# Layer 0 of a relational graph network: eight relation weights made once on the chip, multiplied with scaled sums kept in two buffers

## What is computed

```python
W = jnp.einsum('rb,bde->rde', comp, basis)      # 8 relation weights from 4 bases
h = jnp.einsum('nd,rde->nre', x, W)
msg = h[src, edge_type]
sums = segment_sum(msg, dst * R + edge_type, n * R)
cnt  = segment_sum(ones, dst * R + edge_type, n * R)
agg  = (sums / maximum(cnt, 1)).reshape(n, R, -1).sum(axis=1)
return agg + x @ root + bias
```

## Time and profile before

| what | us |
|---|---|
| median of 3 timed executions | 5880.24 (5867.17 to 5891.92) |
| span of the profiled execution, first to last instruction | 4574.0 |
| layer 0, first to last gather issued | 126.72 to 2251.02 |
| first gather of layer 1 | 2297.41 |
| mean granted TensorE clock (1 is 2.4 GHz) | 0.788 |

### The profile page before, as it was taken

How to read it: one execution, slowest core, us unless ns; L and a number is a source line. 1 busy time by engine, 2 the same in 40 slices (tenths; PEclk the granted TensorE clock), 3 DMA queues, 4 the chain that set the end, 5 groups by cost and what they waited for, 6 DMA issues and landing times.

```text
span 4574.0 us, 121525 instructions
## 1 busy us (share of the span) xinstructions
PE 3738.4 (82%) x38021; PEld 3272.6 (72%) x38022; DVE 3166.8 (69%) x8385; ACT 892.6 (20%) x2493; POOL 3246.8 (71%) x3382
## 2 busy tenths in 40 slices
PE   2476677777767767767549999999999999999999
PEld 2355555555555555555438999999999999999998
DVE  6577677777777777776646767676676767677674
ACT  5000000000000000000003333333333333333333
POOL 1677777777777777777567777777777777777770
PEclk6565665665656656655559999999999999999999
DMA  6666655565555555555466666565656566656661
GB/s 211 181 194 195 174 168 168 165 168 168 165 168 168 164 168 166 167 168 164 122 170 173 173 173 169 170 171 168 169 168 172 167 172 174 170 170 168 171 171 21
DMA packets 359003, 762.96 MB, mean 167 GB/s; under 512 B 130103, under 2 KB 182108, under 8 KB 358657
## 3 DMA queue, kind: packets, MB, share of 16 engines
q0 software_dynamic: 215360, 663.86, 51.3%
q1 hardware_dynamic: 129381, 81.62, 6.6%
q10 hardware_dynamic: 14112, 16.06, 1.0%
HBM read 725.50 MB, written 35.78 MB: 166 GB/s over the span
## 4 chain that ended last, share of the span: by engine, by line
PE 57%; DVE 20%; issue 12%; POOL 6%; DMA 3%; ACT 1%; DVEq 0%; POOLq 0%; SPq 0%; ACTq 0%
PE bank L1469 15%; PE bank L1482 15%; PE bank L1382 12%; DVE mixed L1015 7%; DVE inv L1048 6%; POOL slot L593 5%; PE bank L1414 4%; PE bank L1378 4%; PE bank L1444 3%; PE bank L1445 2%; DVE scaled L1055 2%; DVE hot L1030 2%; DMA slot<-table,idx 2%; DVE inv L1047 1%; DVE mixed L1013 1%
## 5 line engine op out<-in xcount | busy, mean ns | idle before, releaser
L593 POOL DMA_INDIRECT slot<-table,idx x3354 | 3234.9, 965 | 1191.5 <-issue 979.4
L1382 PE MATMUL bank<-hot,slot 128*128 (+1 forms) x21168 | 1252.5, 213 | 62.7 <-DMA slot<-table,idx 54.1
L1382 PEld LDWEIGHTS bank<-hot,slot 128*128 128x128 bf16 x21168 | 1002.3, 108 | 125.2 <-issue 68.6
L1378 PE MATMUL bank<-hot,ones_b 128*128 x1764 | 401.3, 227 | 650.0 <-DVE scaled L1055 225.1
L1378 PEld LDWEIGHTS bank<-hot,ones_b 128*128 128x128 bf16 x1764 | 181.4, 103 | 936.0 <-issue 877.9
L1469 PE MATMUL bank<-root_sb,ffn_w 128*128 128x128 f32 x6272 | 772.9, 278 | 0.0
L1482 PE MATMUL bank<-ffn_w,act 128*128 128x256 f32 x3136 | 756.7, 384 | 1.0 <-DVE root_sb L1142 0.7
L1469 PEld LDWEIGHTS bank<-root_sb,ffn_w 128*128 128x128 f32 x6272 | 741.4, 192 | 8.0
L1482 PEld LDWEIGHTS bank<-ffn_w,act 128*128 128x128 f32 x3136 | 569.5, 190 | 64.9 <-issue 1.1
L1015 DVE SCALAR_TENSOR_TENSOR mixed<-scaled,small,mixed 128x256 f32<-128x256 f32 x1372 | 573.7, 481 | 12.2
L1015 DVE SCALAR_TENSOR_TENSOR mixed<-scaled,comp_sb,mixed 128x256 f32<-128x256 f32 x1372 | 573.4, 480 | 10.5
(11 more groups left out here) (158 smaller groups left out, 2407.5 us busy)
## 6 DMA issues: line engine op xcount, KB each, us to landing
slot<-table,idx POOLq DMA_INDIRECT x3354, 3.1
inv<-inv_d SPq DMA_DIRECT2D x98, 256.0 KB
table<-ffn_w SPq DMA_DIRECT2D x7, 1344.0 KB, 5.5
table<-parts ACTq DMA_DIRECT2D x49, 192.0 KB, 2.9
ffn_w<-in_L_ffn_W_dram SPq DMA_DIRECT2D x16, 512.0 KB, 5.3
typed_x_d<-zn ACTq DMA_DIRECT2D x49, 128.0 KB, 3.2
zn<-in_x_dram SPq DMA_DIRECT2D x48, 128.0 KB
root_sb<-typed_x_d SPq DMA_DIRECT2D x48, 128.0 KB
```

What stands on the lines that cost most here:

```text
L593: gp.indirect_dma_start(out=slot[:, k, :], out_offset=None, in_=table[layer], in_offset=bass.IndirectOffsetOnAxis(ap=idx[:, h, k:k + 1], a ...
L1378: t.matmul(C[:, at], ones_b[:, :], oh, start=(k == 0), stop=(k == TILES - 1), skip_group_check=True)
L1382: last = t.matmul(S[f][:, at], slot[:, k, q * D + f * P:q * D + (f + 1) * P], oh, start=(k == 0 and q == 0), stop=(k == TILES - 1 and q == ...
```

## The change

Three things change in layer 0; layer 1 keeps its mixes.

`make_relations` on DVE, once, after the first two `one_hots`: for each of the eight relations it makes W_r from four bases, by eight products and 24 multiply-adds of 128x512 f32. The bases of layer 0 are loaded into the place of the typed map's weights (`linw_sb`), and the eight results go to `basis_sb` (four), `mixed` (two) and `act` (two), which layer 0 now has free. The typed map's weights are loaded later, after the experts.

`transform` of layer 0 multiplies `scaled` itself with the eight weights: 2 x 2 x (1 + 8) = 36 matmuls in place of 20. It waits for `sc_ready` of its pair in place of `mixed_ready`.

`scale` of layer 0 writes pair p into buffer p & 1 of `scaled` and no longer waits for `mixed_ready`; `mix_bases` is gone from layer 0.

```diff
+            def make_relations():
+
+                dve.wait_ge(basis_in[0], 16)
+                for b in range(NBASIS):
+                    for r in range(R):
+                        s = comp_sb[0][:, r * NBASIS + b:r * NBASIS + b + 1]
+                        w = relation(r, slice(0, HALVES), slice(0, D))
+                        if b == 0:
+                            ins = v.tensor_scalar(w, basis0_sb[:, b, :, :], s, None, ALU.mult)
+                        else:
+                            ins = v.scalar_tensor_tensor(out=w, in0=basis0_sb[:, b, :, :], scalar=s, in1=w,
+                                                         op0=ALU.mult, op1=ALU.add)
+                    if b < NBASIS - 1:
+                        ch.link(ins)
+                ins.then_inc(relations_ready, 1)
...
             def scale(layer, h, G, p, at=0):
                 summed(dve, G, h)
+                at = bass.ds(p & 1, 1) if layer == 0 and not isinstance(p, int) else slice(at, at + 1)
...
                     scale(0, 1, p, p)
                     save(p - 1)
-                    mix_bases(0, p)
                     if more:
                         one_hots(1, p + 1)
                     bias_mask(p)
...
             def transform(layer, G, p):
-                pe.wait_ge(mixed_ready, G + 1)
                 if layer == 0:
+                    pe.wait_ge(relations_ready, 1)
+                    pe.wait_ge(sc_ready, p * 2 + (START + 2))
                     pe.wait_ge(relu_done, START + p)
...
+                            t.matmul(T[:, cols], root_sb[:, 0, k, cols], featT[:, k, bass.ds(p * P, P)],
+                                     start=(k == 0), stop=False)
+                            for r in range(R):
+                                last = t.matmul(T[:, cols], relation(r, k, cols), scaled[:, at, k, r, :],
+                                                start=False, stop=(k == HALVES - 1 and r == R - 1))
```

More of the change, by code:

```diff
@@ L1001, in general_sums, with mix_bases @@
                     assert chg.n == 3
-            def mix_bases(layer, G, first=0, last_=MIXES, at=0):
+            def make_relations():
[12 more added lines that the diff above has]
+                ins.then_inc(relations_ready, 1)
+            def mix_bases(G, first=0, last_=MIXES, at=0):
                 if first == 0:
-                    if not isinstance(G, int) or G > 0:
-                        dve.wait_ge(tr_done, G)
+                    dve.wait_ge(tr_done, G)
                     dve.wait_ge(sc_ready, G * 2 + (START + 2))
@@ L1050, in scale @@
                     dve.wait_ge(inv_in[h], p * 16 + 16)
[L1051 to L1053 removed]
+                if h == 0 and layer == 1:
+                    if isinstance(p, int) and p < 2:
+                        dve.wait_ge(tr_done, PAIRS)
+                    else:
+                        dve.wait_ge(mixed_ready, p - 1)
                 for k in range(HALVES):
                     last = v.tensor_tensor(
[L1056 to L1058 removed]
+                        scaled[:, at, k, :, h * BD:(h + 1) * BD].rearrange("p a r n -> p a n r"),
+                        S[k][:, :].rearrange("p (a n r) -> p a n r", a=1, r=R),
+                        iv.rearrange("p (a n r) -> p a n r", a=1, r=R), ALU.mult)
                 last.then_inc(sc_ready, 1)
@@ L1153, in first_layer @@
                 one_hots(1, 0)
+                make_relations()
                 for h in range(2):
@@ L1213, in body @@
                         if y is not None:
[L1214 removed]
+                            mix_bases(y + PAIRS, first, last_, at)
                         if r is not None:
@@ L1400, in transform @@
             def transform(layer, G, p):
-                pe.wait_ge(mixed_ready, G + 1)
                 if layer == 0:
+                    pe.wait_ge(relations_ready, 1)
+                    pe.wait_ge(sc_ready, p * 2 + (START + 2))
                     pe.wait_ge(relu_done, START + p)
-                elif not isinstance(p, int) or p > 1:
+                    at = slice(p & 1, (p & 1) + 1) if isinstance(p, int) else bass.ds(p & 1, 1)
+                    for o_ in range(HALVES):
+                        cols = slice(o_ * P, (o_ + 1) * P)
+                        for k in range(HALVES):
+                            t.matmul(T[:, cols], root_sb[:, 0, k, cols], featT[:, k, bass.ds(p * P, P)],
[3 more added lines that the diff above has]
+                                                start=False, stop=(k == HALVES - 1 and r == R - 1))
+                    last.then_inc(tr_done, 1)
+                    return
+                pe.wait_ge(mixed_ready, p + 1)
+                if not isinstance(p, int) or p > 1:
                     pe.wait_ge(b2_added, p)
@@ L1414, in transform @@
                             last = t.matmul(T[:, o_ * P:(o_ + 1) * P], basis_sb[:, b, k, o_ * P:(o_ + 1) * P],
-                                            mixed[:, b, k, :], start=(layer == 1 and n == 1),
+                                            mixed[:, b, k, :], start=(n == 1),
                                             stop=(n == NBASIS * HALVES))
```

32 lines of the change are left out of this document (19 added, 13 removed).

## The result

The changed kernel took 6068.06 us (median of 4 executions, 6041.79 to 6073.55) against 5873.7 us before: a ratio of 1.032, with a 95% interval of 1.029 to 1.035. It is slower by 3.2%, above the whole predicted range.

The account below looks back on a forecast made before the run. The prediction took POOL's issuing to bound layer 0 and PE to bound layer 1. Its terms, -23.5 + 0 - 11 + 1 = -33.5 us, took 5880.24 us to 5846.7, predicted as 5847, range 5822 to 5886.

Parts of the forecast that it names:

- Layer 0 is bound by POOL's issuing: Layer 0: POOL never stops, one gather in 1.267 us, 43.4 us a pair, against 40.7 for PE's own chain.
- More matmuls: 0 us in the layer, if PE keeps up: Layer 0's transform: 3.6 us longer, but PE's chain at 42.4 us a pair stays below POOL's 42.9, so 0 us.
- two cases: The 1306 us between span and timed median: outside the program, giving 5846.7 us, or whole program 1.29 times as long, 5837.
- The half microsecond: Layer 0, per pair: the margin by which PE's chain, 42.4 us, was to stay below POOL's 42.9.
- The second rival: Layer 0, block after the transform: PE's chain becomes the bound and the kernel slower, 5976 us; chance 0.12.
- The mixes and POOL: Layer 0: without the mixes' multiply-adds the mean gather falls from 0.963 to 0.949 us, 23.5 us less.
- The gap: Between the layers: the last transform waits for the scaled sums, not the mixes, and starts earlier: -11 us.
- The start: Before the first `scale`: `make_relations` takes 20 us inside DVE's idle time, some 16 gathers may be longer: +1 us.
- The register for p & 1: Layer 0, PE and DVE: the buffer's register address, set ahead, is hidden behind matmuls that wait for the array.

Follow-up runs that it names:

- e0: The kernel before, unchanged, profiled once more for a trace of an execution like the timed ones: 5863.96 us.
- e1: The changed kernel with only four of the eight relations multiplied in layer 0, 20 matmuls per transform: 5863.85 us, ratio 0.9963 to the kernel before.
- e5: The changed kernel with PE's loop of layer 0 over pairs in place of blocks, no branch inside: 6041.59 us, ratio 1.0182 to the kernel before.
- e2: The changed kernel with the transform's 32 relation matmuls moving 64 columns in place of 128: 6150.16 us, ratio 1.0454 to the kernel before.

## Why the prediction was wrong

**The step that failed is the first: "Layer 0 is bound by POOL's issuing", and with it "More matmuls: 0 us in the layer, if PE keeps up".** The profile showed POOL never waiting, in an execution 1306 us shorter than the timed ones. I wrote that no row says where those 1306 us lie, and then priced two cases, all outside the program or all spread evenly. They lay in neither. From the first profile to e0 PE's issue rose from 212 to 893 us in layer 0 and from 2 to 388 in layer 1 (some of it waits that lost their releaser), and PE's busy time by 401 us over the whole, at a lower granted clock (0.57 for 0.60 and 0.92 for 0.98); waits for gathers became less. With that a pair takes PE's chain 54.4 us before the change and 58.4 after it, where I had 43.0 (40.7 without waits for gathers) and 42.4. POOL's 42.9 is hidden: it waits 592 us for PE. The half microsecond on which the argument stood did not exist in the timed executions.

**The net cost came out near the price by chance; the zero was wrong.** I had 3.6 us per transform at the higher clock, which is 176 us over 49 pairs, and layer 0 grew by 187. But the parts are not those of the sum. The transform grew by 8.2 us (9.8 in e0, 18.0 after, means over 47 pairs): 53% of its relation steps go at 0.21 us and not at 0.11, and stops stand in it. Of that 4.3 came back: the tiles of both blocks were 1.7 us shorter, and the waits for `scale` and before the transform 2.6.

**The second rival had the mechanism and the wrong threshold.** "PE's chain becomes the bound" was given 5976, because it was to begin at 10.6 us for a transform. PE's chain already was the bound, so what the transform adds net counted from the first.

**The mixes and POOL: the mechanism held, the gain did not.** In e0 the 365 gathers that lie mostly beside the mixes' multiply-adds take 1002 ns in the mean, the 577 with no DVE instruction beside them 945. The mean gather is 949 ns without the mixes and 959 with them, so 18 of the predicted 23.5 us of POOL's work did go; but POOL waits for PE, and e1 shows nothing of it in layer 0. As for the Trainium skill's page SBUF — State Buffer, section Who interferes with whom, whose inference would leave the gathers alone: these traces disagree with it, by 0.06 us for a gather beside the mixes, and no time hangs on it here.

**The gap: -7.5 for -11, and -13.7 in e1.** The transform starts without its 17.6 us of waiting. The last one takes 4.3 us longer (6.5 in e0, 10.8 after) in place of 3.6; the rest of what is missing is that the block before it ended 3.6 us later behind the last gather than in e0, and in e1 it did not. **The start: 0 for +1**, with 19.5 us for `make_relations` where I took 20. The register for p & 1, taken as hidden, can't be told from nothing (e1).

## What to carry to other kernels

Before a sum is made from a profile, its span must be held against the timed median: where the two differ by a fifth, the profile is of another execution, and what it shows as the bound may not be the bound. When no explanation of the difference has a row, profile again before you price anything, or give the engines that look second as much weight as the first. Work moved from an engine with idle time to the one that sets the pace is paid for, here with 0.2 us net for each matmul. And a wait listed without a releaser may be a gap in the record: look at what ended just before it on the other engines before a mechanism is built on it.

## What the runs showed of the hardware

In e0's trace the instructions of PE's and SP's sequencers come in steps of about 0.70 us or its multiples where no semaphore is waited for. Steps of 0.6 to 6 us to an instruction that waits for no semaphore (gathers left out): 567 on PE (525 us) and 432 on SP in layer 0. In layer 0 of the first profile of the same program there is none on PE or SP. This looks like instructions that arrive too slowly, but that is argued, not shown. The queues of kind "instruction" moved 16 and 24 packets in the whole changed kernel, and 127 and 23 in the first profile and in e0 alike; in e0 none of them lies between 272 and 2837 us, while PE stops all along. No run took the stops away. The Trainium skill's page Runtime: NRT & Kernel Launch, section Instruction fetch mechanics, says that a taken branch to code outside what is held forces a fetch before execution goes on; no run here shows such a fetch in the loop, and e5, with fewer branches, was 0.3% faster only. Another rival is untested: the two executions of the same program were not recorded alike (74,403 and 33,837 semaphore updates), and no run tells whether the recording has a part in the stops. Why the first profile has none, and what they are, stays open.

The other surprise is e2: f32 matmuls of 64 columns followed each other at the same steps as those of 128, 0.213 us at the lower clock and 0.11 at the higher, and the granted clock was 0.50 through a whole transform (1543.7 to 1551.7 and 1556.6 to 1563.9 in its trace). Layer 0 became 90 us longer, at 0.53 in place of 0.61.
